# Layer 1 of a two-layer decoder: the down projection in half precision, squares added by GpSimd, and new step orders

## What is computed

```python
def _mamba2(x, ...):                       # end of the Mamba block
    ...
    y = y * jax.nn.silu(z)
    y = y * lax.rsqrt(jnp.mean(y * y, axis=-1, keepdims=True) + 1e-05) * norm_w
    return y @ out_proj_w.T
...
def _binarize(w):
    alpha = jax.lax.stop_gradient(jnp.mean(jnp.abs(w), axis=1, keepdims=True))
    bw = alpha * jnp.sign(w)
    return w + jax.lax.stop_gradient(bw - w)
bw1 = _binarize(w1)
h = jnp.einsum('bsd,hd->bsh', x, bw1) + b1
h = jax.nn.gelu(h, approximate=False)
bw2 = _binarize(w2)
out = jnp.einsum('bsh,dh->bsd', h, bw2) + b2
...
x = _layernorm(x + _L1_ffn_ref(x, ...), axis=-1)
```

## Time and profile before

| | us |
|---|---|
| runs | 1304.98, 1305.52, 1308.28 |
| median | 1305.52 |
| the profiled execution, its own time | 1298.92 |
| its span in the profile | 1297.2 |
| layer 1 in it | from about 862 to the end |

### The profile page before, as it was taken

How to read it: one execution, slowest core, us unless ns; L and a number is a source line. 1 busy time by engine, 2 the same in 40 slices (tenths; PEclk the granted TensorE clock), 3 DMA queues, 4 the chain that set the end, 5 groups by cost and what they waited for, 6 DMA issues and landing times.

```text
span 1297.2 us, 22848 instructions
## 1 busy us (share of the span) xinstructions
PE 1187.7 (92%) x8404; PEld 988.4 (76%) x8404; DVE 830.5 (64%) x2630; ACT 648.9 (50%) x1363; POOL 153.4 (12%) x184
## 2 busy tenths in 40 slices
...
DMA packets 21388, 33.27 MB, mean 26 GB/s; under 512 B 11424, under 2 KB 12192, under 8 KB 20128
## 3 DMA queue, kind: packets, MB, share of 16 engines
...
## 4 chain that ended last, share of the span: by engine, by line
PE 74%; DVE 13%; ACT 8%; issue 3%; POOL 1%; DVEq 0%; ACTq 0%; POOLq 0%
PE ps L504 41%; PE ps L747 6%; PE ps L645 4%; PE ps L663 2%; PE ps L662 2%; DVE z L1589 2%; DVE arena L1779 2%; PE ps L661 2%; DVE arena L1406 2%; PE ps L637 1%; PE ps L635 1%; PE ps L608 1%; ACT L1263 1%; PE ps L621 1%; PE ps L886 1%
## 5 line engine op out<-in xcount | busy, mean ns | idle before, releaser
L504 PE MATMUL ps<-arena,wts 128*128 128x256 f16 (+1 forms) x1344 | 189.2, 295 | 20.6 <-ACTq L477 20.6
L504 PE MATMUL ps<-wts,arena 128*128 128x256 f32 (+2 forms) x1008 | 201.0, 357 | 3.8 <-ACT arena L1347 3.2
L504 PEld LDWEIGHTS ps<-arena,wts 128*128 128x128 f16 (+1 forms) x1344 | 153.2, 115 | 49.1 <-issue 20.5
L504 PEld LDWEIGHTS ps<-wts,arena 128*128 128x128 f32 (+1 forms) x1008 | 154.6, 155 | 41.3 <-ACT arena L1347 4.0
L1589 DVE SCALAR_TENSOR_TENSOR z<-ps,small,z 128x256 f32<-128x256 f32 x256 | 123.9, 484 | 41.3 <-PE ps L747 26.8
L1197 ACT ACTIVATE pq<-ps 128x512 f32<-128x512 f32 x72 | 43.0, 598 | 169.1 <-PE ps L504 169.0
L747 PE MATMUL ps<-wts,pq 128*128 128x256 f32 x512 | 120.8, 380 | 6.2 <-DVE z L1589 6.2
L747 PEld LDWEIGHTS ps<-wts,pq 128*128 128x128 f32 x512 | 92.6, 190 | 18.7 <-DVE z L1589 4.9
L645 PE MATMUL ps<-ident,pq 128*128 128x128 f32 x384 | 73.9, 306 | 33.1 <-DVE arena L1506 12.3
L1106 ACT ACTIVATE pq<-pq,nms 128x128 f32<-128x128 f32 x128 | 50.9, 398 | 92.1 <-DVE nms L1479 92.1
L1477 DVE CUSTOM_DVE_ANT_0 pq<-ps,mb 128x128 f32<-128x128 f32 x128 | 36.6, 286 | 86.0 <-PE ps L637 85.7
...
## 6 DMA issues: line engine op xcount, KB each, us to landing
cT<-in_cT SPq DMA_DIRECT2D x16, 256.0 KB, 2.7
wts<-in_up SPq DMA_DIRECT2D x1, 2304.0 KB, 15.5
...
xT<-in_xT SPq DMA_DIRECT2D x8, 256.0 KB, 4.0
xin<-in_x SPq DMA_DIRECT2D x8, 256.0 KB, 2.9
xmid<-xin SPq DMA_DIRECT2D x8, 256.0 KB, 2.0
...
```

The source lines that it names most:

```text
L504: ins = mm(out_, l, r, start=(n == 0), stop=(n == len(pairs) - 1))
```

## The change

- The Gelu now writes into a new float32 buffer `gl` (one for both sequences, four slots of two blocks). ScalarE then waits for its own Gelu and copies the 128x512 values to half precision (`hh`); GpSimd subtracts that copy from `gl` and writes the rest in half precision (`hl`). `down` waits for the four `hl` and multiplies both parts by the bare signs, held in half precision (`w2h`): 32 half-precision matmuls instead of 16 in float32. A Gelu waits until GpSimd has read its slot of `gl` for the sequence before.
- The scale of the rows (`al2r`) is applied behind the projection: `ffn_out` multiplies the PSUM result by it, then adds the residual, two 128x512 DVE instructions instead of one.
- GpSimd adds the four blocks of squares to one (a 128x512 and a 128x256 addition a sequence, step `sq` in its list); `rms` on PE is two matmuls instead of eight.
- All five order lists are new. ScalarE's list in layer 1 has 53 table loads, where it had 70. In SP's list `1.ctx.1` (the load of the context for turn 1) now stands ahead of `3.x.0`, `0.store.1` ahead of `2.ctx.0`, and `1.store.1` ahead of `3.ctx.1`.

```diff
 PE_ORDER = steps("""
...
-    3.cell.1.0 3.score.1.0 3.up.0.0 3.up.0.6 3.score.1.1 3.read.1.0 3.read.1.1 3.up.0.2 3.up.0.4 3.down.0
...
+    3.read.0.1 3.ztb.1 2.ztc.1 3.gates.1 2.up.1.2 2.up.1.6 2.up.1.4 3.gain.1 2.up.1.0 3.rows.1 3.cell.1.0
+    3.cell.1.1 2.down.1 3.score.1.0 3.cols.1 3.ztc.0 3.up.0.0 3.read.1.0 3.score.1.1 3.up.0.6 3.read.1.1
...
 POOL_ORDER = steps("""
-    0.load.0 0.load.1 1.load.0 1.load.1 2.load.0 2.load.1 0.ztc.0 3.load.0 0.ztc.1 1.ztc.0 3.load.1 1.ztc.1
-    2.ztc.0 2.ztc.1 3.ztc.0 3.ztc.1""")
+    0.load.0 0.load.1 1.load.0 1.load.1 0.sq.0 0.sq.1 2.load.1 2.load.0 0.ztc.0 1.sq.0 1.sq.1 0.ztc.1 0.up.0.2
...
         def hTb(s):
-            return carve_m(s)[5]
+            return flat(carve_m(s)[5])
+
+        def hTh(s):
+            return hTb(s).bitcast(F16).rearrange("p (i m t) -> p i m t", i=2, m=FM)
...
+        w2h = flat(w2T).bitcast(F16)[:, 0:FM * C].rearrange("p (m c) -> p m c", m=FM)
...
             def mamba_rms(s):
 
                 ysq = carve_m(s)[4]
-                for m in range(0, DM, 2):
-                    eng.wait_ge(*pe.at("ysq", s, m))
+                eng.wait_ge(*pe.at("yss", s))
                 o = take(("ss", s), ("ss", s, "out"))
                 for t in range(TT):
-                    ins = group(o[:, t:t + 1], [(ysq[:, m, t * P:t * P + P], onesq[:, 0:1]) for m in range(DM)])
+                    ins = mm(o[:, t:t + 1], ysq[:, 0, t * P:t * P + P], onesq[:, 0:1], start=True, stop=True)
                 ins.then_inc(*pe.up(("ss", s)))
 
...
+            def ffn_down(s):
+                for m in range(0, FM, 2):
+                    eng.wait_ge(*pe.at("hl", s, m))
+                o = take(("f2", s), ("f2", s, "out"), spot(RINGS["b"]))
+                for t in range(TT):
+                    ins = group(o[:, t * C:t * C + C], [(hTh(s)[:, i, m, t * P:t * P + P], w2h[:, m, :])
+                                                        for m in range(FM) for i in range(2)])
+                ins.then_inc(*pe.up(("f2", s)))
...
-                    rowproj(s, "f2", w2T, hTb(s), [("f1", s, m, "out") for m in range(0, FM, 2)], spot(RINGS["b"]), kc=FM)
+                    ffn_down(s)
...
                     m = n[1]
                     eng.wait_ge(*act.at("f1", s, m))
+                    if (turn, s) > (TURNS, 0):
+                        eng.wait_ge(*act.reached(((turn, "hl", 0, m) if s else (turn - 1, "hl", NS - 1, m))))
                     for j in range(2):
-                        A(hTb(s)[:, m + j, :], psv(("f1", s, m))[:, j * T:j * T + T], ACT.Gelu,
+                        A(gl[:, m // 2, j * T:j * T + T], psv(("f1", s, m))[:, j * T:j * T + T], ACT.Gelu,
                           scale=al1[:, m + j:m + j + 1], bias=b1[:, m + j:m + j + 1]).then_inc(
                             *act.up(("f1", s, m, "out") if j else None))
+                    eng.wait_ge(*act.own())
+                    A(flat(hTh(s)[:, 0, m:m + 2, :]), gl[:, m // 2, :], ACT.Copy).then_inc(*act.up(("hh", s, m)))
...
             def scaled_signs(cc):
                 eng.wait_ge(*v.at("wT", 1, cc, 0))
-                V_.tensor_tensor(w2T[:, cc, :], psv(("wT", 1, cc, 0))[:, 0:C], al2r, ALU.mult).then_inc(
-                    *v.up(("wT", 1, cc, 0, "out")))
+                V_.tensor_copy(w2h[:, cc, :], psv(("wT", 1, cc, 0))[:, 0:C]).then_inc(*v.up(("wT", 1, cc, 0, "out")))
...
             def ffn_out(s):
+                y = hTb(s)[:, 0:TT * C]
+                eng.wait_ge(*v.at("f2", s))
+                V_.tensor_tensor(y.rearrange("p (t c) -> p t c", t=TT), psv(("f2", s)).rearrange("p (t c) -> p t c", t=TT),
+                                 rowb(al2r, C), ALU.mult).then_inc(*v.up(("f2", s, "out")))
                 eng.wait_ge(*v.at("z5b", s))
-                eng.wait_ge(*v.at("f2", s))
-                V_.tensor_tensor(z2[s][:, :, :], psv(("f2", s)).rearrange("p (t c) -> p t c", t=TT), z2[s][:, :, :],
-                                 ALU.add).then_inc(*v.up(("f2", s, "out")))
+                eng.wait_ge(*v.own())
+                V_.tensor_tensor(flat(z2[s][:, :, :]), y, flat(z2[s][:, :, :]), ALU.add).then_inc(*v.up())
...
+                if step == "sq":
+                    s = n[0]
+                    ysq = carve_m(s)[4]
+                    for m in range(0, DM, 2):
+                        eng.wait_ge(*po.at("ysq", s, m))
+                    G.tensor_tensor(flat(ysq[:, 0:2, :]), flat(ysq[:, 0:2, :]), flat(ysq[:, 2:4, :]), ALU.add).then_inc(
+                        *po.up())
+                    eng.wait_ge(*po.own())
+                    G.tensor_tensor(ysq[:, 0, :], ysq[:, 0, :], ysq[:, 1, :], ALU.add).then_inc(*po.up(("yss", s)))
+                if step == "up":
+                    s, m = n
+                    eng.wait_ge(*po.at("hh", s, m))
+                    G.tensor_tensor(flat(hTh(s)[:, 1, m:m + 2, :]), gl[:, m // 2, :], flat(hTh(s)[:, 0, m:m + 2, :]),
+                                    ALU.subtract).then_inc(*po.up(("hl", s, m)))
```

More of the change, by code:

```diff
@@ L102 @@
-    2.gain.0 3.decay.0.3 2.rows.0 3.scan.0.2 2.rms.1 3.decay.0.1 3.in.1.0 2.cols.0 3.in.1.4 2.cell.0.0
-    2.score.0.0 3.zg.1.2 3.scan.0.0 3.dsum.1 2.ztb.1 3.zg.1.0 2.read.0.0 3.csrow.1 3.cb.1 3.xs.1 1.read.1.0
-    3.scan.0.3 3.decay.1.2 3.decay.1.3 1.down.0 2.gates.1 2.cell.0.1 3.scan.1.2 2.score.0.1 1.ztc.1 3.scan.0.1
-    3.scan.1.3 3.decay.1.0 3.decay.1.1 1.up.1.0 2.gain.1 2.read.0.1 2.rows.1 3.rms.0 1.up.1.2 2.cols.1
-    2.cell.1.1 3.out.0 2.score.1.1 3.scan.1.0 2.cell.1.0 1.up.1.6 2.score.1.0 2.read.1.1 3.ztb.0 3.scan.1.1
@@ L107 @@
-    1.up.1.4 3.gates.0 2.read.1.0 2.ztc.0 1.down.1 2.up.0.0 3.gain.0 3.rms.1 3.rows.0 2.up.0.4 2.up.0.6 3.cols.0
-    3.cell.0.0 3.score.0.0 2.up.0.2 3.out.1 3.cell.0.1 2.down.0 3.read.0.0 3.ztb.1 3.score.0.1 2.ztc.1 3.gates.1
-    3.read.0.1 2.up.1.0 2.up.1.2 3.gain.1 2.up.1.6 2.up.1.4 3.rows.1 2.down.1 3.cell.1.1 3.ztc.0 3.cols.1
-    3.cell.1.0 3.score.1.0 3.up.0.0 3.up.0.6 3.score.1.1 3.read.1.0 3.read.1.1 3.up.0.2 3.up.0.4 3.down.0
-    3.ztc.1 3.up.1.6 3.up.1.4 3.up.1.0 3.up.1.2 3.down.1""")
@@ new lines @@
+    0.scan.0.2 0.decay.1.0 0.decay.1.3 0.scan.0.1 0.decay.1.2 0.scan.1.1 1.dsum.0 0.scan.1.0 1.dt.1 1.csrow.0
+    -.tr.1.4.0 -.tr.1.3.0 0.rms.0 0.scan.1.2 0.scan.1.3 0.out.0 1.dsum.1 1.in.0.2 1.zg.0.2 0.ztb.0 0.rms.1
+    1.in.0.0 0.gates.0 1.csrow.1 0.out.1 1.in.1.2 1.xs.0 1.in.1.0 0.gain.0 1.zg.1.2 0.rows.0 0.ztb.1 1.zg.0.0
+    1.in.0.4 0.cell.0.1 0.score.0.1 1.zg.1.0 1.in.1.4 0.gates.1 1.xs.1 1.cb.0 0.read.0.1 0.cols.0 1.decay.0.1
+    1.decay.0.0 0.gain.1 2.load.1 1.scan.0.1 1.decay.0.2 2.dt.1 1.scan.0.0 0.rows.1 0.cell.0.0 1.cb.1
@@ new lines @@
+    0.score.0.0 2.load.0 1.scan.0.2 0.read.0.0 0.cell.1.0 0.score.1.0 1.decay.1.0 2.dt.0 1.decay.1.2 1.scan.1.0
+    0.read.1.0 0.cols.1 1.decay.1.1 0.cell.1.1 1.scan.1.2 0.score.1.1 1.decay.0.3 1.scan.1.1 1.decay.1.3
+    0.read.1.1 0.ztc.0 1.scan.0.3 2.dsum.0 1.scan.1.3 2.dsum.1 1.out.0 1.rms.0 2.zg.0.2 1.rms.1 2.in.0.0
+    0.up.0.6 0.up.0.2 2.in.0.4 2.csrow.0 2.csrow.1 0.ztc.1 2.in.0.2 1.ztb.0 0.up.0.0 1.out.1 2.in.1.2 0.up.1.2
+    0.up.1.0 2.in.1.0 1.gates.0 1.ztb.1 2.zg.1.0 2.in.1.4 1.gates.1 1.gain.0 0.up.0.4 2.xs.1 1.rows.0 0.up.1.6
@@ new lines @@
+    2.cb.0 2.xs.0 2.zg.1.2 0.down.0 2.decay.0.0 1.cell.0.0 2.zg.0.0 1.gain.1 1.cell.0.1 1.cols.0 1.rows.1
+    2.scan.0.0 0.up.1.4 1.score.0.1 1.cell.1.0 1.score.1.0 1.read.0.1 0.down.1 2.decay.0.2 2.decay.0.1
+    1.read.1.0 1.score.0.0 1.cell.1.1 2.scan.0.2 2.scan.0.1 1.score.1.1 3.load.0 2.cb.1 1.read.0.0 3.dt.0
+    2.decay.1.0 1.cols.1 1.read.1.1 2.decay.1.1 2.decay.1.2 2.scan.1.0 2.decay.0.3 2.decay.1.3 3.load.1
+    2.scan.0.3 2.scan.1.2 3.dt.1 2.scan.1.3 2.out.0 2.rms.0 3.in.0.0 3.zg.0.2 3.in.0.4 3.zg.0.0 3.in.0.2 2.ztb.0
@@ new lines @@
+    2.scan.1.1 1.ztc.0 1.ztc.1 2.gates.0 3.dsum.1 1.up.0.2 3.xs.0 1.up.0.6 3.dsum.0 1.up.0.0 1.up.0.4 2.gain.0
+    3.csrow.0 2.rows.0 1.up.1.6 2.rms.1 2.out.1 2.cell.0.0 2.score.0.0 3.in.1.2 1.up.1.0 1.up.1.4 3.in.1.0
+    2.ztb.1 2.cols.0 3.csrow.1 3.cb.0 3.in.1.4 2.gates.1 3.decay.0.2 1.down.0 3.decay.0.0 3.decay.0.3 3.zg.1.2
+    3.decay.0.1 3.scan.0.0 3.xs.1 3.scan.0.2 3.zg.1.0 2.read.0.0 2.gain.1 2.cell.0.1 2.rows.1 3.scan.0.1
+    1.up.1.2 3.cb.1 2.score.0.1 2.cols.1 3.scan.0.3 2.read.0.1 3.decay.1.0 3.decay.1.2 3.out.0 2.cell.1.0
```

139 lines of the change are left out of this document (66 added, 73 removed).

## The result

The changed kernel took 1319.69 us (median of 4 executions, 1313.58 to 1324.24) where the kernel before took 1305.25 (1298.93 to 1308.28) beside it: ratio 1.0114, 95% interval 1.0057 to 1.0171. The forecast was 1280 us, faster. It is slower, by 1.1%. The prediction took 0.3% for what a measurement can tell; with four executions the interval is 0.6% to either side.

What follows compares the result with a forecast made beforehand. TensorE was taken to bound layer 1's first 391 us, a serial chain the last 35. Terms -31.8 + 0.2 + 1 + 2 + 3 + 2 - 2 = -25.6 us took the median from 1305.5 to 1279.9, predicted 1280; range 1263 to 1297.

Steps and rivals of the forecast that it cites:

- the first part: Layer 1 from 871 to 1262 us, TensorE-bound: six down and eight rms shortened there save 31.8 us.
- contention: VectorE slowed by GpSimd on shared SBUF interfaces: 10 us of stretched work, 2 us of it reaching TensorE.
- about 39 us of work: TensorE's busy time from 871 us to the end falls from 402 to about 363 us.
- +1 + 2 + 3 + 2: Costs: Gelu runs +1, last down of turn 2 +2, waiting for GpSimd's additions +3, VectorE contention +2 us.
- VectorE has 87 us free: VectorE is busy 303.6 of the first part's 391.0 us, leaving 87 us free beside contention.
- -2 us, between 0 and -10: Clock in the first part: fewer one-column matmuls shorten slow-clock runs, a gain of 2 us.
- +1 us: Runs of four up: a Gelu pair with copy takes 1.68 us, so TensorE can outrun ScalarE; cost 1 us.
- set-off of copies against table loads: On ScalarE, 32 copies add 19.9 us and 17 fewer table loads remove 21.8, so its sum stays about 280.
- VectorE and ScalarE become the bound: Rival: VectorE 93% busy under full contention, half the gain lost, about -13 us, 1292 us; 18%.
- +3 us: rms waits for GpSimd's additions, 8 x 1.9 = 15 us, a quarter uncovered: 3 us (0 to 15).
- The rival with the uncovered link: Each rms and down waits uncovered for GpSimd, stretched 1.3 times by contention: +12 us, 1318 us; 6%.
- The end chain: Last 35 us, serial: the last down's gain goes into copy, subtraction and second VectorE instruction; +0.2 us.

Runs made afterwards that it cites:

- relief alone: Kernel before, old lists, only TensorE's work cut: half-precision down, two matmuls per rms; no copy, GpSimd step or second VectorE instruction (low half, scales left out): 0.9798, repeated 0.9822.
- the old lists: Changed kernel's arithmetic with the five order lists of the kernel before, GpSimd's new steps put in by the producers' order: 1319.5 us mean, ratio 1.0145.
- the folded scale: Kernel with activations rounded by the Gelu, row scales folded into the half-precision weights, one VectorE instruction behind down: 1296.8 us mean, ratio 0.9951.
- rounded activations: Kernel before, old lists, Gelu rounding to half precision itself, 16 matmuls per down, two VectorE instructions behind it, no copy or GpSimd work: 1301.1 us mean, ratio 0.9977.
- bfloat16 squares: The kernel with the folded scale, plus squares written in bfloat16, 8 matmul instructions per sum in place of 16: 1295.9 us mean, ratio 0.9942.
- unwaited: Relief alone plus copy and VectorE instruction, plus all GpSimd additions and subtractions, which TensorE does not wait for: 1308.9 us mean, ratio 1.0049.
- copy and VectorE instruction: Relief alone plus ScalarE's 32 copies that down waits for and the scale as a second VectorE instruction, no GpSimd step: 1304.1 us mean, ratio 1.0015.

## Where the prediction was wrong

*What held.* The durations of all added and removed instructions, but the small addition (a `down` at full clock takes 3.66 us, forecast 3.5); TensorE as the engine whose relief pays: measured alone, -25.5 us of rest where the first part's sum had -31.8; contention of 9 us on VectorE; and that GpSimd is rarely the engine waited for. That TensorE would lose about 39 us of work held in full-speed work only: by the matmul and clock records it fell from 375.2 to 339.5 us from 871 us on. The busy time, which the prediction forecast at 363 us, is 388.4, since more of it is at half clock.

*The step that failed most: what is put on the other engines, "+1 + 2 + 3 + 2", 8 us in all.* From relief alone (1279.6 us in the mean of both) to the changed kernel (1319.3) it is 40 us: 29 of rest and 11 of clock loss. The second VectorE instruction was put at nothing in the first part; alone it cost 16 us. The prediction reasoned that VectorE has 87 us free and that ScalarE's sum stays the same, so that added work is covered.

*The clock, "-2 us, between 0 and -10".* The clock loss grew by 13 us in the changed kernel and by 22 with the old lists. I took the one-column matmuls as what lowers the clock, and so their removal as a gain. The runs don't bear that out: relief alone, with a quarter of the one-column matmuls, has a clock loss of 80 us (mean of both) against 78, and half of them gone changed nothing beside the folded scale. So it isn't relief as such that cost the clock here; the loss came with what was added behind it, and in the kernels with rounded activations with the smaller `down`. One place shows a wait among narrow matmuls with a low clock behind it. Stretches of the changed kernel, columns as in the earlier trace rows:

```profile
1232.00:1236.00 4.00, 4.00 (x28) 3.40 (x27) 3.76 (x10) 0.93 (x5) 0.00 (x0) 1.00 0.00 0
1236.00:1240.00 4.00, 2.48 (x12) 1.81 (x11) 3.86 (x13) 2.45 (x8) 0.00 (x0) 0.87 0.06 24
1240.00:1244.00 4.00, 2.79 (x13) 2.52 (x12) 3.07 (x12) 0.50 (x2) 0.00 (x0) 0.50 0.11 44
1244.00:1256.00 12.00, 11.92 (x57) 10.04 (x58) 8.14 (x36) 6.25 (x14) 1.83 (x2) 0.50 0.00 1
```

What TensorE did there, of its timeline:

```profile
1235.58 0.39 PE L947 MATMUL ps<-wts,pq 128*128 128x65 f32 x2
...
1237.09 0.38 PE L932 MATMUL ps<-zT,cT 64*128 64x128 f32 x2
1238.99 1.22 PE L931 MATMUL ps<-zT,cT 64*128 64x256 f32 x2 [1.52 <-DVE small L1891]
1240.00 0.63 PE L932 MATMUL ps<-zT,cT 64*128 64x128 f32 x2
1241.84 0.66 PE L945 MATMUL ps<-wts,pq 128*128 128x65 f32 x2 [1.21 <-issue]
```

Matmuls of 65 columns, a wait of 1.52 us for VectorE, and at its end the clock is at half; it stays there over a second wait of 1.21 us and through 12 us in which TensorE is busy for 11.92, the last 4.7 of them with matmuls of 256 columns (from 1251.32 on). In these 12 us alone 6 us of full-speed work are lost. The Trainium skill, TensorE: Matmul & The Clock Gate, section What's actually happening, lets the clock follow how busy TensorE has been. That fits the fall after the wait, but not the 12 busy us at half clock behind it. It doesn't easily tell the last two stretches above apart, of the relieved kernel and of that with bfloat16 squares: busy shares of 370.91/405.9 = 0.91 and 379.31/429.4 = 0.88 are close. But the slower clock lengthens the busy time itself: in full-speed work the shares are 336.7/405.9 = 0.83 and 322.3/429.4 = 0.75, so the runs don't decide this.

*Within the 8 us: "+1 us" for the Gelu runs and the sum's silence on the rest of ScalarE's and VectorE's lists.* "Its sum stays, about 280 us, but in some 360 us instead of 391", I wrote, and charged 1 us. The 20 us of copies, put on the old lists, cost 11 us of rest, waited for or not. ScalarE is busy there for 292.6/405.9 = 72% of the time and VectorE for 314.2/405.9 = 77% (the relieved kernel's row above), and yet ScalarE's list passed on about half of what was put into it, VectorE's 2 of 5.5 us, and each much more with the clock. Taking the table loads out again with the new lists gave nothing back (they differ in much else), so the prediction's set-off of copies against table loads failed as well. The rival "VectorE and ScalarE become the bound" saw this mechanism, but gave it 13 us and no clock.

*And "+3 us" for the GpSimd link.* Waited for, it cost 11 us more than unwaited, 3 of them rest and 8 clock loss. The rival with the uncovered link was nearest to the time (1318) by luck, and wrong on the place: apart from 0.7 us ahead of one `rms`, only two waits of 3.9 us name GpSimd.

*The end chain, "+0.2".* The last subtraction ends at 1309.16 + 1.15 = 1310.3, 7.6 us behind the first Gelu at 1302.69 (forecast 8.0), but most of the last `down` runs at half clock and takes 5.33 us:

```profile
1302.69 1.02 ACT L1365 ACTIVATE wts<-ps,wts 128x256 f32<-128x256 f32 x2 [1.41 <-PE ps L512]
...
1309.16 1.15 POOL L2136 TENSOR_TENSOR arena<-wts,arena 128x512 f16<-128x512 f32 x1 [0.42 <-ACT arena L1369]
...
1310.36 5.33 PE L512 MATMUL ps<-wts,arena 128*128 128x256 f16 x32 [3.91 <-POOL arena L2136]
1315.74 0.69 DVE L1961 TENSOR_TENSOR arena<-ps,wts 128x512 f32<-128x512 f32 x1 [15.03 <-PE ps L512]
1316.53 0.69 DVE L1965 TENSOR_TENSOR z<-arena,z 128x512 f32<-128x512 f32 x1
```

From the first Gelu to the residual it takes 14.5 us, against 13.0 before: +1.5.

*The sum by rungs*, in means: relief -23.2 us, copy and VectorE instruction +24.5, GpSimd's work +4.8, its link +10.6, new lists -0.2: +16.5 us (1302.8 to 1319.3). Forecast: -25.6. What a rung costs depends on the order in which they are added; the second VectorE instruction cost 16 us on relief alone, the copy 18, both together 25.

*What stays open.* Why 5.5 us of VectorE work cost 14 us of clock on the relieved kernel, and only 4 us in all where activations are rounded (1301.1 with it, 1296.8 where the scale is folded). Why copy and instruction together cost 25 us and not 34. And what it is that lowers the clock: waits, the smaller share of wide matmuls, or both. No run changes one of these alone. The new lists' 0 or so on the new arithmetic is also a sum, of 9 us more rest and 9 less clock loss, over four and five executions only.
